# Block transposes on VectorE behind the value product, and x, queries and first feed-forward product for two batches at a time

## What is computed

```python
def attention(x, kv, W, n_keys):          # the reference, condensed
    q, k, v = x @ Wq + bq, kv @ Wk + bk, kv @ Wv + bv      # per head: 16 columns
    p = softmax(q @ k.T / 4)                               # mask in L0, causal in SELF
    return (p @ v) @ Wo + bo

x = LN(attention(x, ctx) + x)             # L0, masked
x = LN(attention(x, ctx) + x)             # L1
x = x + attention(ln(x), ln(x))           # SELF, causal, 256 keys
x = x + attention(ln(x), ctx)             # CROSS
x = x + relu(ln(x) @ f_w1 + f_b1) @ f_w2 + f_b2            # FFN, 1024 wide
x = x + attention(ln(x), ctx, ternary weights)             # L3
```

## Time and profile before

| | before |
|---|---|
| median of 3 runs | 1398.24 us (1395.89 to 1398.70) |
| the profiled execution | 1397.33 us, its span 1395.6 us |
| PE, DVE, ACT, POOL busy | 1329.5, 994.2, 898.1, 603.0 us |
| granted TensorE clock, mean | 0.995 |
| DMA | 35.11 MB, mean 25 GB/s |

### The profile page before, as it was taken

One profiled execution on the slowest core, in us unless ns is written; L12 is line 12 of the kernel. 1 busy time (PEld: TensorE's weight loads), 2 busy tenths in 40 slices (PEclk: granted clock), 3 DMA queues, 4 the chain that ended last, 5 costly groups with the idle time before them and its releaser, 6 DMA issues.

```text
span 1395.6 us, 46148 instructions
## 1 busy us (share of the span) xinstructions
PE 1329.5 (95%) x20076; PEld 1138.8 (82%) x20076; DVE 994.2 (71%) x1842; ACT 898.1 (64%) x1519; POOL 603.0 (43%) x767
## 2 busy tenths in 40 slices
PE   5999999999999999999999999999999999899997
PEld 4777888777887878888788878888999999778885
DVE  4778777888788777767776788886664446767774
ACT  4777777777777756666566776776434435667764
POOL 4944544576644643443334342222686665111100
PEclk9999999999999999999999999999999999999999
DMA  7211100010100000000000110000000000001000
GB/s 283 76 31 35 31 13 10 24 31 25 38 9 9 10 25 3 3 2 2 3 2 25 33 31 16 9 9 24 9 9 1 2 1 15 10 32 39 17 25 32
DMA packets 16609, 35.11 MB, mean 25 GB/s; under 512 B 2071, under 2 KB 7447, under 8 KB 15895
## 3 DMA queue, kind: packets, MB, share of 16 engines
q1 hardware_dynamic: 16407, 32.16, 7.1%
HBM read 27.96 MB, written 4.19 MB: 23 GB/s over the span
## 4 chain that ended last, share of the span: by engine, by line
PE 67%; DVE 14%; ACT 8%; POOL 5%; issue 3%; DMA 2%; SPq 0%; DVEq 0%; POOLq 0%; ACTq 0%
DVE s_nm L1101 9%; PE ps L717 8%; PE ps L782 8%; PE ps L744 6%; PE ps L796 6%; PE ps L810 6%; PE ps L606 5%; PE ps L659 5%; PE ps L761 5%; PE ps L631 4%; ACT s_PU L952 4%; PE ps L618 4%; PE ps L595 2%; PE ps L722 2%; DVE s_KH L1058 2%
## 5 line engine op out<-in xcount | busy, mean ns | idle before, releaser
L1101 DVE TENSOR_REDUCE s_nm<-ps 128x8 fp32r<-128x960 f32 (+1 forms) x352 | 395.8, 1168 | 88.4 <-PE ps L659 51.0
L952 ACT ACTIVATE s_PU<-ps 120x1024 f32<-120x1024 f32 (+1 forms) x288 | 280.6, 1024 | 105.5 <-PE ps L722 105.3
L717 PE MATMUL ps<-s_Qs,s_KH 32*120 32x256 f32 (+2 forms) x4608 | 184.8, 288 | 6.4 <-ACT s_PU L952 2.6
L1225 POOL TENSOR_TENSOR s_xs<-s_xs,s_rowv 128x512 f32<-128x512 f32 x96 | 123.9, 1291 | 151.8 <-ACT s_nt L857 133.6
L717 PEld LDWEIGHTS ps<-s_Qs,s_KH 32*120 32x120 f32 (+1 forms) x4608 | 151.5, 181 | 28.4 <-issue 5.1
L1254 POOL TENSOR_SCALAR s_rs<-s_mv 128x2 f32<-128x2 f32 x96 | 23.2, 242 | 325.4 <-DVE s_mv L1138 319.8
L961 ACT ACTIVATE s_Os<-ps 128x512 f32<-128x512 f32 x160 | 95.0, 598 | 102.8 <-PE ps L744 64.2
L782 PE MATMUL ps<-s_W,s_oT 128*128 128x256 f32 x960 | 135.3, 291 | 5.2 <-DVE s_oT L1030 3.5
L606 PE MATMUL ps<-s_xT,s_W 128*128 128x256 f32 x960 | 135.9, 292 | 3.1 <-POOL s_xT L1231 2.8
L744 PE MATMUL ps<-s_PU,s_Vp 120*32 120x256 f32 x2048 | 129.5, 384 | 9.2 <-ACT s_PU L952 7.2
L782 PEld LDWEIGHTS ps<-s_W,s_oT 128*128 128x128 f32 x960 | 120.0, 190 | 16.8 <-DVE s_oT L1030 7.0
(11 more groups left out here) (96 smaller groups left out, 2554.4 us busy)
## 6 DMA issues: line engine op xcount, KB each, us to landing
s_cf<-ctx_t SPq DMA_DIRECT2D x32, 240.0 KB, 2.6
s_ws<-weights SPq DMA_DIRECT2D x28, 256.0 KB, 2.7
s_nt<-x_t SPq DMA_DIRECT2D x16, 256.0 KB, 2.6
s_xs<-x_nat SPq DMA_DIRECT2D x4, 1024.0 KB, 11.3
out<-s_xs SPq DMA_DIRECT2D x16, 256.0 KB, 2.0
s_rowv<-rows SPq DMA_DIRECT2D x6, 512.0 KB, 3.9
s_mi<-mask SPq DMA_DIRECT2D x8, 120.0 KB, 3.4
s_who<-who SPq DMA_DIRECT2D x1, 128.0 KB, 3.2
```

The source lines that it names most:

```text
L717: e.matmul(banks[j][0:n, wide * x:wide * x + wide], kz[row[j], lk, g, c, k0:k0 + n], q[row[j], lq, g, qs_], start=(x == 0 and y_ == 0), st ...
L952: t = e.activation(P_of(i, k)[0:n, :, :], pair("B", i, k)[0:n, :, :], ACT.Exp, scale=0.25)
L1101: e.tensor_reduce(o, v, AX.X, ALU.max, negate=True).then_inc(sem["max"])
L1225: e.tensor_tensor(xs[:, b, :, :], xs[:, b, :, :], row2(layer, 0), ALU.add).then_inc(sem["pool"])
```

## The change

Behind the value product, X (DVE) transposes PV's PSUM bank into `Os` in blocks of 32 by 32: within each block, 32 queries go down and one head's 32 entries across. ONe (DVE) makes one reciprocal of 32 sums and one product of 512 columns for the whole item, in place in `Os`. OT (DVE) turns the 16 values of each head back by two block transposes of 256 columns into `On` (SBUF). PVe, ON and the old OT are gone; OTh and OTl read `On`. The rows of `oT` come out in another order of heads, and the output weights are reordered for that outside the kernel (`mixed`).

T, Th, Tl, Q, Qh, Ql are made once for the two batches of a pair: T is eight transposes and Q 12 products of 512 columns, both into two banks. F1 is four units for a pair, each of 12 products of 512 columns and one matrix of weights; Fa and Fv are one instruction each in place of two; F2 is four units with the same products as before.

Also changed: the weights have ten places handed out matrix by matrix (Wh waits for the readers of the matrix ten earlier); buffers (Os 3 halves to 2 whole, oT 2 to 1, K0 2 to 1, Q 3 to 4); K of L3 comes behind the last F1, K and V items keep their order; the tables `WANT`, `LONG` and `STAY`, and so the order of all lists.

```diff
-WSLOT = {n: k % 3 for k, n in enumerate(SETS)}
+MATRICES = [(n, m) for n in SETS for m in range(4)]
+PLACE = {x: k % 10 for k, x in enumerate(MATRICES)}
...
+            if i == pair:
+                add("PE", "T", after=ready, rings=[("S", ("T", i, 0), [("Tl", i, 0)]), ("xT", i, users)])
+                add("ACT", "Th", after=[("T", i, 0)])
+                add("DVE", "Tl", after=[("Th", i, 0)])
...
+            if i == pair:
+                add("PE", "Q", after=[x_t, (rest_of(layer), layer, 0)],
+                    rings=[("S", ("Q", i, 0), [("Ql", i, 0)])] + [("Q", x, [("B", x, u) for u in range(units(x))]) for x in two])
...
-                    rings=[("S", ("F1", i, u), [("Fv", i, 2 * u), ("Fv", i, 2 * u + 1)]), ("PU", ("F", i, u), [("Hl", i, u)]),
+                    rings=[("S", ("F1", i, u), [("Fv", i, 2 * u + 1)]), ("PU", ("F", i, u), [("Hl", i, u)]),
...
+                behind = [("F1", 5 * B - 2, 3)] if layer == "L3" else []
...
-                add("ACT", "PVe", hf, after=[("PV", i, hf)])
-                add("PE", "ON", hf, after=[("PVe", i, hf)],
-                    rings=[("MI", ("ON", i, hf), [("ONe", i, hf)])] + ([] if hf else [("On", i, [("OT", i, 0)])]))
-                add("DVE", "ONe", hf, after=[("ON", i, hf)])
-            add("PE", "OT", after=[("ONe", i, 0), ("ONe", i, 1)], rings=[("MI", ("OT", i, 0), [("OTl", i, 0)]), ("oT", i, [("O", i, 0)])])
+                add("DVE", "X", hf, after=[("PV", i, hf)])
+            add("DVE", "ONe", after=[("X", i, 0), ("X", i, 1)])
+            add("DVE", "OT", after=[("ONe", i, 0)], rings=[("On", i, [("OTl", i, 0)]), ("oT", i, [("O", i, 0)])])
...
-                            t = e.matmul(m[:, g * 256:g * 256 + 256], wv(layer, cw, 0)[:, k, 128 * g:128 * g + 128], xT_of(i)[:, cx, k, :],
+                            t = e.matmul(v[:, g, :], wv(layer, cw, 0)[:, k, 128 * g:128 * g + 128], xT_of(i)[:, cx, k, :],
...
+            def X(i, hf):
+                was = ring["Os"].before[i]
+                if was is not None:
+                    w.wait_ge(sem["OT"], nth("OT", was))
+                w.wait_ge(sem["PV"], nth("PV", i, hf))
+                o = Os[slot("Os", i)][:, 2 * hf:2 * hf + 2, :, :].rearrange("p g m c -> p (g m c)")
+                e.transpose(o, bankM("PV", i, hf)).then_inc(sem["X"])
+            def ONe(i):
+                n, o = nth("ONe", i), Os[slot("Os", i)][:, :, :, :].rearrange("p g m c -> p (g m) c")
+                w.wait_ge(sem["X"], max(nth("X", i, hf) for hf in range(2)))
+                rc = Rc[:, :].rearrange("p (h o) -> p h o", o=1)
+                e.reciprocal(rc, o[:, :, 16:17]).then_inc(sem["R"])
+                w.wait_ge(sem["R"], n)
+                e.tensor_tensor(o[:, :, 0:16], o[:, :, 0:16], rc.to_broadcast([128, 32, 16]), ALU.mult).then_inc(sem["ONe"])
+            def OT(i):
+                w.wait_ge(sem["ONe"], nth("ONe", i))
+                o = Os[slot("Os", i)]
+                for hf in range(2):
+                    t = e.transpose(On[slot("On", i)][:, hf, :], o[:, 2 * hf:2 * hf + 2, :, 0:16].rearrange("p g m c -> p m g c"))
+                t.then_inc(sem["OT"])
```

More of the change, by code:

```diff
@@ L17 @@
 MANY = {"MI": 1, "S": 2}
[L20 to L33, removed]
@@ L44 @@
 TURN = .19
-STAY = 0.236
+STAY = 0.462
 NEXT = .11
@@ L256, in make_plan @@
             else:
                 add("ACT", "N", after=[x_ready(i), ("rs", i - B, 1 if layer_of(i - B) == "L1" else 0)],
[L258 to L259 removed]
+                    rings=[("nt", i, [("T", pair, 0)])])
                 add("POOL", "bo", after=[("N", i, 0), ("row", nr, 0)])
[L261 to L263 removed]
+                ready = [("N", x, 0) for x in two]
@@ L276, in make_plan @@
-            last = ("F2", i, 1)
-        else:
-            add("PE", "Q", after=[x_t, (rest_of(layer), layer, 0)],
-                rings=[("MI", ("Q", i, 0), [("Ql", i, 0)]), ("Q", i, [("B", i, u) for u in range(units(i))])])
-            add("ACT", "Qh", after=[("Q", i, 0)] + ([("wa", layer, 0)] if FOLDED[layer] else []))
-            add("DVE", "Ql", after=[("Qh", i, 0)])
+                add("PE", "F2", u, after=[("Hl", i, u), ("Wl", "F2", u)] + ([("F2", i, u - 1)] if u else []),
+                    rings=[] if u else [("MI", ("F2", x, 0), [("y", x, 0)]) for x in two])
@@ L282, in make_plan @@
+            last = ("F2", pair, 3)
+        else:
+            if i == pair:
+                add("PE", "Q", after=[x_t, (rest_of(layer), layer, 0)],
+                    rings=[("S", ("Q", i, 0), [("Ql", i, 0)])] + [("Q", x, [("B", x, u) for u in range(units(x))]) for x in two])
+                add("ACT", "Qh", after=[("Q", i, 0)] + ([("wa", layer, 0)] if FOLDED[layer] else []))
+                add("DVE", "Ql", after=[("Qh", i, 0)])
             if own:
@@ L306, in make_plan @@
                     add("DVE", "max", 2 * u + q, after=[("A", i, u)])
+            for u in range(1, units(i)):
+                p.stages["A", i, u].after.append(("A", i, 0))
             add("PE", "M", after=[("max", i, k) for k in range(2 * units(i))],
@@ L378, in make_plan @@
                 last = ("wg", layer, m)
-            p.add("ACT", "Wh", layer, m, want=at, after=[last] + before)
+            was = had_place(layer, m)
+            p.add("ACT", "Wh", layer, m, want=at, after=[last] + (readers(*was) if was else []))
             if layer == "L0":
@@ L894, in Qhi @@
             def Qhi(i):
-                m, was = bankM("Q", i), ring["Q"].before[i]
-                if was is not None:
-                    w.wait_ge(sem["B"], max(nth("B", was, u) for u in range(units(was))))
+                v = pair("Q", i, 0)
+                for was in (ring["Q"].before[i], ring["Q"].before[i + 1]):
+                    if was is not None:
+                        w.wait_ge(sem["B"], max(nth("B", was, u) for u in range(units(was))))
                 w.wait_ge(sem["Q"], nth("Q", i))
@@ L992, in Whi @@
             def Whi(n, m):
-                before = SETS.index(n) - 3
-                if before >= 0:
-                    w.wait_ge(sem["O"], max(nth("O", B * LAYERS.index(SETS[before]) + b) for b in range(B)))
+                was = had_place(n, m)
+                if was is not None:
+                    last = readers(*was)
+                    w.wait_ge(sem[last[0][0]], max(nth(*x) for x in last))
                 if m in FOLDED[n]:
```

310 lines of the change are left out of this document (151 added, 159 removed).

## The result

| | before | after |
|---|---|---|
| median | 1398.41 us (1395.89 to 1398.70) | 1444.96 us (1442.16 to 1447.45) |
| profiled execution, its span | 1397.33, 1395.6 us | 1444.29, 1442.6 us |
| TensorE busy / idle within the span | 1329.5 / 66.1 us | 1276.4 / 166.2 us |
| granted TensorE clock, mean | 0.995 | 0.955 |

A forecast was written before the change was run, and what follows sets the result against it. TensorE bounded the kernel before; afterwards VectorE would bound L0, L1 and CROSS. Layer paces times 16 batches plus fixed parts gave 1277 us (TensorE alone) to 1323 us (VectorE in those layers); 1305 us was chosen, range 1268 to 1350.

The forecast's parts named there:

- The bound of the kernel before: Whole kernel: TensorE, busy 95% of the span, sets the pace everywhere; VectorE is busy 71%.
- VectorE's new work: Attention batches: X, ONe and OT in, old pairs out, a net 1.55 us more per batch; VectorE busy about 1110 us.
- the 1824 records: TensorE: no ON and OT, Q and F1 halved, 960 + 480 + 384 matmul records fewer than 20076.
- the pace of L1 and CROSS where VectorE is full: L1 and CROSS: VectorE at 96% asks for 13.1 and 12.7 us per batch.
- Rival 3: VectorE's f32 block transposes take two cycles a column, making the kernel slower than before: 1429 us; chance 0.10.
- 1277: Whole kernel: the time in us if TensorE alone counts.
- 1323: Whole kernel: the time in us if VectorE sets L0, L1 and CROSS stage by stage.
- rival 2: Chain from PV to O on full VectorE: TensorE waits for O, idle share doubles, 45 us more: 1350 us; chance 0.11.
- 20 us gained: Q and F1 on TensorE: half as many products at 20 ns each, together 20 us less.
- 2 us lost at the start: Start: joint Q behind both inputs and Ql twice as long add 2 us (0 to 4).
- rival 4: Q and F1: 512-column products cost as two of 256, 20 us of TensorE time stay: 1315 us; chance within the forecast's 0.60.

The follow-up runs named there:

- e12: The kernel of e7 with only its tables WANT and STAY fitted once more: 1384.76 us.
- e1: The changed kernel, waits and order kept, with X, ONe and OT cut to a small part of their columns: 1407.85 us.
- e4: The kernel before with only X, ONe and OT on VectorE (Os 2, oT 1), T, Q and F1 per batch, order refitted: 1416.59 us.
- e7: The kernel of e4 with a second On buffer and tables fitted for that: 1393.44 us.
- e11: The kernel of e7 with its tables but one On buffer: 1394.82 us.
- e5: The changed kernel with PVe, ON and OT back on ScalarE and TensorE, joint T, Q and F1 kept, order refitted: 1404.88 us.
- e8: The kernel of e7, same order, with X, the product of ONe and OT cut to 32 columns: 1348.02 us.
- e6: The changed kernel with only the numbers in WANT, LONG and STAY fitted anew to measured durations: 1427.97 us.
- e10: The kernel of e4 with its own tables and On in two buffers: 1415.18 us.
- e9: The kernel of e7, same order, with four extra 256-column products on TensorE ahead of M's wait: 1397.68 us.
- e3: The changed kernel with four extra 256-column bf16 products on TensorE ahead of M's wait: 1444.98 us.

## Why the prediction was wrong

**Right.** The bound of the kernel before; VectorE's new work (X 0.63 us from start to start against 0.65, OT 0.67 for both halves, 358.22 to 358.89, against 0.76, ONe 0.97, 356.31 to 357.28, against 1.0, busy 1115 against 1110); the 1824 records; the pace of L1 and CROSS where VectorE is full, as e12 shows for the blocks alone. That the busy total came out so near is in part luck: by the distances given, X, ONe and OT are 0.16 us per batch cheaper than forecast (13 us in all), and slow instances of L1130 and L1040 put back some 20 (means of 860 and 775 ns, medians of 692). Rival 3, two cycles a column, is out by the 702 and 417 ns. The Trainium skill ("VectorE: DVE Perf Modes", The three transpose paths) spoke against the change by 311 ns for 128 columns of bf16; read as a rate that would be 1244 ns for 512 columns, an estimate from that page. The f32 transposes of this case take 702.

**Wrong, first: the weaving of two nearly full engines.** The span of 1303 us forecast for the profiled execution holds 1329.5 - 124 = 1205 us of TensorE's work and so 98 us of idle. Measured were 166. The prediction wrote that two engines at 97% seldom mesh by an order fixed beforehand, and then gave that no term of its own: it only chose between 1277 and 1323, and for 1323 it took each stage at 96% of its fuller engine, a share that stood for one full engine beside one at 82%. It put this case into rival 2, at a chance of 0.11 and at 1350 us, and named the chain from PV to O as its cause; a time above before's it gave only to rival 3. The runs show less of that chain than of the order: with VectorE's load gone (e1) TensorE idles 140 us, and with other tables and the same instructions (e4's to e7's, e11) 118 in place of 135, 22 us less time. Waits for OTl (L802) are 11.4 of the 166 us. The blocks bring the idle time (e4 135 us, e5 72), and the best order found for them still has 121 (e12); with VectorE's load taken off the order of e7, 95 are left of 118 (e8). Whether a better order would remove it or the waits between the stages keep it, no run shows.

**Wrong, second: the granted clock was in no term.** TensorE's busy total should have fallen by 124 us and fell by 53. With full and half speed as its levels, a mean of 0.955 means 9% of the span at half speed, about 130 us; work that fills it would have taken 65 us at full speed. Before, 0.995 makes it 7. The difference, 58 us, is an estimate from above, since part of the slow time is idle. By the spread of executions within a kernel, 0.7 to 1.4 us for 0.001, the 0.040 are 28 to 56 us. So the clock accounts for a good part, up to four fifths, of the 71 us by which busy time exceeds the 1205. Idle time (+68) and busy time (+71) together are the 139 us between 1303 and 1442.6. The profile before gave the hint that was passed over: it stands at 1.00 in every stretch of the earlier trace rows, with TensorE at 96% or more. None of its rows shows what a TensorE that waits more often is granted. In after the idle share alone doesn't tell either: at 88% busy in SELF the clock stayed at 1.00, at 92% in L1 it was 0.93.

**Wrong, third: moves that cost nothing.** The joint Q and T were put at 20 us gained and 2 us lost at the start. A joint Q takes 2.89 us against 2 x 1.53 by V's row, 0.17 x 40 = 7 us; a unit of F1 0.14 us less than in the earlier trace rows, 32 x 0.14 = 4.5 us; that makes 11 in place of 20, so rival 4 was half true. And e5, which has this gain alone, is 0.5% slower than before in the one order tried for it. What costs there is not shown: its joint T and Q and its F1 have some 3 us of idle time before them in all. At the start the loss is not 2 us: 1.4 batches by 100 us are some 18, part of it at a clock of 0.81. The same count in the other runs takes it apart. By 100 us before has done 5.9 batches, e4 (blocks, without the pairs) 1124/190 = 5.9, e5 (pairs) 1080/196 = 5.5, e6 (all of the change in another order) 984/184 = 5.3, after 4.5. So some half a batch, 5 to 8 us, goes with the pairs, and more than that with after's order.

**Not priced, and in part not tested.** That Os, oT and K0 lose a buffer had no term. e10 and e11 show that a second On, a buffer the change doesn't take away, is worth 1.4 us. For Os, oT and K0 no run shows it; nor was a second On tried in the full change.

What stays open: why TensorE idles 118 to 121 us with the blocks even in the better orders (66 before), and how much of after's 60 us over e12 is the pairs and how much is that no good order was found for them. e6 against e4, both with fitted tables, are 11 us apart, and e5 against before 8 us; both point to the pairs costing some 10 us, but each has an order of its own, and e10 and e12, which differ in their tables alone, lie 30 us apart.

## What to carry to other kernels

When a change moves work from the bound engine to one that it makes nearly as full, price the meshing too: here TensorE's idle time went from 66 us to 118 or more in every order tried for the blocks. Another order for the same instructions gave 17 us (e6), 22 us (e4 to e11) and 9 us (e7 to e12), and none gave what was forecast. Compare parts of a change only with an order refitted for each, and test a buffer with the order held. Ask what the forecast idle time does to TensorE's clock: its mean fell by 0.04 here, which by the estimates above cost some 28 to 58 us, against 124 us of work taken away.

## What the runs showed of the hardware

- A VectorE transpose in blocks of 32 by 32 on f32, from PSUM to SBUF, goes at the pace of the other one-pass operations: 702 ns for 128x512 and, from SBUF to SBUF, 417 ns for 128x256.
- Two waits of 0.53 and 1.19 us within 2.7 us, in the middle of a dense stretch, were followed by 7 us at a granted clock of 0.51. Between 100 and 400 us before has single waits of 1.2 and 1.3 us, and the clock stands at 1.00 there in every stretch of 100 us.
- Executions of one kernel differ in their mean granted clock, and the time goes with it: e9 took 1391.67 us at 0.983 and 1407.04 at 0.972, e3 1439.94 at 0.972 and 1454.17 at 0.958.
- Three VectorE operations with two inputs in SBUF have slow instances: the product at L1130 takes 692 ns at the median and up to 1816, OTl (L1040) 692 at the median and up to 1781, where it took at most 693 when it read PSUM, and Kl (L1067) 710 and up to 1801. With one input in SBUF, the transpose L1140 stays within 394 to 446 ns and the statistics L1160 within 376 to 429. The cause wasn't tested; GpSimd is busy 43% of the span beside them.
- VectorE's added load costs where it stands, not by the engine's share: reductions behind ON that kept it busy for 67 us more cost 27 us at a VectorE of 75%.
